# Attention score products in 32-row array tiles, row maxima by small transfers, batches run on without a break

## What is computed

```python
p = jnp.sum(c * up[None], axis=-1); z = jnp.sum(c * uz[None], axis=-1)
P = jax.nn.sigmoid(p) * key_len
Z = jax.nn.sigmoid(z) * key_len
G = -(j[None, None, None, :] - P[..., None]) ** 2 * 2.0 / Z[..., None] ** 2
scores = jnp.einsum('bhqd,bhkd->bhqk', q, k) / jnp.sqrt(jnp.float32(D))
scores = scores + G
probs = jax.nn.softmax(scores, axis=-1)
ctx = jnp.einsum('bhqk,bhkd->bhqd', probs, v)
```

## Time and profile before

| | |
|---|---|
| time, median of 3 runs | 1984.03 us |
| profiled execution, from first to last instruction | 1977.9 us |
| PE busy | 1562.8 us (79%) |
| DVE busy | 1303.5 us (66%) |
| ACT busy | 806.1 us (41%) |
| POOL busy | 344.8 us (17%) |
| first score product | 174.4 us |
| last context written | 1026.8 us |

### The profile page before, as it was taken

The page is one execution under the profiler, slowest core; times in us unless marked ns, Lnnn a source line. Parts: engine busy times, 40 slices in busy tenths (PEclk is TensorE's granted clock), DMA queues, the critical chain, the costliest instruction groups (busy, mean ns, idle before and its releaser), DMA issues. The chain is left out here.

```text
span 1977.9 us, 27765 instructions
## 1 busy us (share of the span) xinstructions
PE 1562.8 (79%) x8393; PEld 1008.6 (51%) x8393; DVE 1303.5 (66%) x2889; ACT 806.1 (41%) x979; POOL 344.8 (17%) x522
## 2 busy tenths in 40 slices
PE   4579999999999999999986804530077687999998
PEld 2245555455554555555544503420055466888887
DVE  3668888788887888788807893319754344666665
ACT  1123666566665666666673300000043333333432
POOL 0422111111111111110012203530410230000000
PEclk9867999999999999999998855555578898999999
DMA  2051000000000000000000105527000000000000
GB/s 55 0 206 50 1 1 1 2 1 1 1 1 2 1 1 1 1 1 1 1 10 22 53 11 119 129 58 289 15 0 0 1 0 1 6 7 11 6 5 11
DMA packets 38686, 53.75 MB, mean 27 GB/s; under 512 B 6032, under 2 KB 23808, under 8 KB 38555
## 3 DMA queue, kind: packets, MB, share of 16 engines
q1 hardware_dynamic: 35995, 47.62, 7.0%
q0 software_dynamic: 2560, 4.55, 1.4%
HBM read 32.93 MB, written 20.97 MB: 27 GB/s over the span
## 5 line engine op out<-in xcount | busy, mean ns | idle before, releaser
L657 DVE TENSOR_REDUCE mx<-psum 128x1 f32<-128x512 f32 x1024 | 649.1, 685 | 144.8 <-PE psum L507 144.5
L611 ACT ACTIVATE probs<-psum 128x1024 f32<-128x1024 f32 x512 | 505.1, 1024 | 312.6 <-PE psum L529 312.5
L507 PE MATMUL psum<-akT,aqT 128*128 128x512 f32 x1024 | 403.4, 446 | 5.6 <-ACT akT L592 4.7
L529 PE MATMUL psum<-aqT,akT 128*128 128x512 f32 x1024 | 331.6, 407 | 7.7 <-issue 6.2
L507 PEld LDWEIGHTS psum<-akT,aqT 128*128 128x128 f32 x1024 | 185.6, 194 | 235.9 <-DVE mx L657 160.0
L542 PE MATMUL psum<-probs,vaug 128*32 128x512 f32 x2048 | 272.8, 605 | 0.8 <-ACT probs L611 0.4
L529 PEld LDWEIGHTS psum<-aqT,akT 128*128 128x128 f32 x1024 | 186.7, 190 | 81.4 <-ACT probs L611 28.4
L2146 ACT ACTIVATE sil<-psum,moe_bg 128x512 f32<-128x512 f32 x128 | 88.0, 688 | 205.8 <-PE psum L2100 205.7
L2235 DVE SCALAR_TENSOR_TENSOR hid<-psum,moe_bu,sil 128x512 f32<-128x512 f32 x128 | 95.9, 750 | 86.4 <-ACT sil L2146 82.9
L464 POOL CAST akT<-kstage 32x512 fp32r<-32x512 f32 x120 | 73.3, 611 | 323.1 <-ACT kstage L595 317.7
L2084 PEld LDWEIGHTS psum<-down,hid 128*128 128x128 f32 x1024 | 123.6, 192 | 6.9 <-issue 1.5
(11 more groups left out here) (276 smaller groups left out, 2147.4 us busy)
## 6 DMA issues: line engine op xcount, KB each, us to landing
pick_rows<-zeros SPq DMA_DIRECT2D x48, 256.0 KB, 3.7
yk<-pick_rows SPq DMA_DIRECT2D x8, 1536.0 KB, 8.7
token_rows<-xrow SPq DMA_DIRECT2D x8, 512.0 KB, 2.8
w1b<-in_w1T SPq DMA_DIRECT2D x8, 352.0 KB
w3b<-in_w3T SPq DMA_DIRECT2D x8, 352.0 KB
w2b<-in_w2T SPq DMA_DIRECT2D x8, 352.0 KB
X<-in_x SPq DMA_DIRECT2D x4, 512.0 KB, 7.7
out<-acc SPq DMA_DIRECT2D x8, 256.0 KB, 2.3
```

The lines of the kernel that those rows point to most:

```text
L507: last = e.matmul(bank[:], qT[u % NG][:, i * P:(i + 1) * P], kT[u % NG][:, h, c * 512:(c + 1) * 512], start=True, stop=True)
L529: last = e.matmul(scores[:, n % 2, j, :], kT[g][:, h, kt * P:(kt + 1) * P], qT[g][:, hf * QH:(hf + 1) * QH], start=True, stop=True)
L611: a.activation(probs[:, n % 4, :, :], scores[:, n % 2, :, :], ACT.Exp)\
L657: dve.reduce_max(mx[:, i, h, c:c + 1], bank[:], X_AXIS).then_inc(tp_free, 1)
```

## The change

It does these things:
- `kT[u]` becomes [128, 1024], like `qT`. A score product or an X of head h takes rows 32h to 32h + 31 of both operands, so it is put into one of the array's four groups of 32 rows and uses that alone. The spreading by POOL, `kstage`, the clearing of `kT` (4 x 128 x 4096 numbers) and of `mrow` go. ACT copies K straight to `kT`.
- The X of a unit begin three steps earlier (LEAD = 3): each step has exactly four, of heads 2, 0, 3, 1, at 0.1, 0.3, 0.7 and 0.8 of the step. The last is placed 3.2 steps before the unit's scores begin, M 2.95 steps before them.
- M is one transpose of 128 x 64 to 64 x 128; ACT copies it to `mT`, and SP sends it with four transfers (one for each head, 16 pieces of 512 bytes each) to rows 30 and 31 of that head in `qT`. DVE's two additions of 128 x 512 go. The unit's first score waits for the transfers (`m_in`).
- Batches are joined: the last values and the last C of a batch stand in the first steps of the next, and the X of the next go on. The prologue has unit 0's 64 X, M, and the first 12 X of unit 1.
- SP issues three zero fills after each unit's four transfers instead of 48 at once. Counters start at 0.

```diff
-        def maxima(at, u):
-            return [(at + (2 * j + c) * 0.23, "X", u, (j // TB, j % TB, c))
-                    for j in range(GH * TB) for c in range(2)]\
-                + halves(at + 14.9, "M", u)
...
+        def maxima(v, steps):
+            lo = STEPS * (v - 1) - LEAD
             out = []
...
+            for j in range(GH * TB * 2):
+                k, r = divmod(j, 4)
+                if k in steps:
+                    out.append((lo + k + (0.1, 0.3, 0.7, 0.8)[r], "X", v, ((2, 0, 3, 1)[r], k // 2, k % 2)))
+            return out
+
+        def operands_of(v):
+            at = STEPS * (v - 2)
+            return [(at + 3.2 + 1.5 * i, "QQKK"[i], v, i % 2) for i in range(4)]
+
+        def maxima_turned(v):
+            return [(STEPS * v - LEAD + 0.05, "M", v, None)]
+
+        def context_turned(u):
+            return [(8 * u + 10.4, "C", u, None)]
...
+            with sp.Fori(0, B) as b:
+                for u in range(NG):
+                    sp.wait_ge(m_copied, b * NG + u + 1)
+                    for h in range(GH):
+                        sp.dma_start(
+                            f32(qT[u][h * R + 30:h * R + 32, :]).rearrange("l (i q) -> l i q", i=TB),
+                            f32(mT[u % 2][h * 2 * TB:(h + 1) * 2 * TB, :])).then_inc(m_in, 16)
+                    for z in range(PER):
+                        sp.dma_start(rows[:, bass.ds(((b * NG + u) * PER + z) * W, W)], zeros[:])\
+                            .then_inc(zeroed, 16)
...
+                    r = slice(h * R, (h + 1) * R)
+                    last = e.matmul(bank[:], qT[u % NG][r, i * P:(i + 1) * P],
+                                    kT[u % NG][r, c * 512:(c + 1) * 512], start=True, stop=True)
+                elif kind == "M":
+                    e.wait_ge(dve_own, (b * NG + u + 1) * M_STEPS)
+                    stand_alone(e)
+                    last = e.transpose(bank[0:GH * 2 * TB, 0:P],
+                                       f32(mrow[:]).rearrange("p h l i -> p (h l i)"), t["ident"][:])
...
-                    last = e.matmul(scores[:, n % 2, j, :],
-                                    kT[g][:, h, kt * P:(kt + 1) * P], qT[g][:, hf * QH:(hf + 1) * QH],
-                                    start=True, stop=True)
+                    r = slice(h * R, (h + 1) * R)
+                    last = e.matmul(scores[:, n % 2, j, :], kT[g][r, kt * P:(kt + 1) * P],
+                                    qT[g][r, hf * QH:(hf + 1) * QH], start=True, stop=True)
...
+                for k in range(BS):
+                    if k % STEPS == 0:
+                        e.wait_ge(m_in, (b * NG + k // STEPS + 1) * 16 * GH)
+                    score_step(b, 2 * k, first)
+                    events_to(k + 0.25)
+                    score_step(b, 2 * k + 1, first)
                     events_to(k + 0.6)
-                    if k:
-                        values_step(b, k - 1)
+                    if k or not first:
+                        values_step(b, k - 1, first)
                     events_to(k + 1)
```

More of the change, by code:

```diff
@@ new lines, in batch_events @@
+        def batch_events(first, last):
+            out = [] if first else context_turned(-1)
+            out += maxima(1, LATE) + maxima_turned(1)
+            for g in range(2, NG + 2):
+                if g < NG or not last:
+                    out += operands_of(g)
+            for g in range(2, NG):
+                out += maxima(g, ALL) + maxima_turned(g)
+            if not last:
+                out += maxima(NG, ALL) + maxima_turned(NG) + maxima(NG + 1, EARLY)
+            for u in range(2 * NG - 1):
+                out += context_turned(u)
+            if last:
+                out += [(BS + 1, "C", 2 * NG - 1, None)]
+            elif not first:
+                out += [(30.01, "-", None, None)]
+            return out
@@ L452, in build @@
[L452 to L465, removed]
@@ L565, in batch @@
                     events_to(k + 0.6)
[L566 to L567 removed]
+                    if k or not first:
+                        values_step(b, k - 1, first)
                     events_to(k + 1)
[L569 to L576 removed]
+                if last:
+                    values_step(b, BS - 1, first)
+                    events_to(BS + 2)
@@ L615, in batch @@
-                    if n % 2 and n // 2 % 8 == 0 and n > 1:
-                        context(b, n // 16 - 1)
-                context(b, 2 * NG - 1)
-            first = Events(FIRST)
-            for n, x in enumerate(FIRST):
-                if x[1] in "QK":
-                    operands(0, first, n)
-            with a.Fori(0, B - 1) as b:
-                batch(b, False)
-            batch(B - 1, True)
+                    while turns and ring.events[turns[0]][0] < k + (1 if n % 2 else 0.25):
+                        operands(b, ring, turns.pop(0))
@@ new lines, in event @@
+            def event(b, ring, n):
+                _, kind, u, at = ring.events[n]
+                bank = tp[ring.bank(n)]
+                if kind == "M":
+                    last = max(m for m in range(n) if ring.events[m][1] == "X" and ring.events[m][2] == u)
+                    dve.wait_ge(tp_free, ring.emptied(last))
+                    if ring.after is not None:
+                        dve.wait_ge(m_copied, b * NG + u)
+                    s = Steps(dve, dve_own, (b * NG + u) * M_STEPS)
+                    s.do(dve.tensor_tensor(rowmax[:], mx[:, :, :, 0], mx[:, :, :, 1], ALU.max))
+                    s.do(dve.tensor_copy(mrow[:, :, 0, :], rowmax[:]))
+                    s.done(dve.tensor_tensor(mrow[:, :, 1, :], rowmax[:], f32(mrow[:, :, 0, :]), ALU.subtract))
+                    assert s.n == M_STEPS
+                elif kind == "C":
+                    dve.wait_ge(tp_full, ring.full(n))
```

320 lines of the change are left out of this document (148 added, 172 removed).

## The result

The changed kernel takes 2009.95 us (median of 1998.7 to 2022.2) beside 1984.42 us of the kernel before in the same comparison: 1.0131 times as long, interval 1.0079 to 1.0184. The forecast was 1892 us. The profiled execution has a span of 1996.9 us against 1977.9. Of the four executions two took 1999 and 2000 us at a mean granted clock of 0.798 and 0.797, two 2020 and 2022 us at 0.786; the trace is of the fastest.

What follows compares the result with a forecast made beforehand. A loop over three banks was to bound the step at 2.70 us: 640 us, with Q, K, C, M, tail and ends 771.5 from a first score at 163.7; 92 us less gives 1892 us, own range 1860 to 1915, 1840 to 1980 at 81%.

Steps and rivals of the forecast that it cites:

- The loop of 2.70 us: Plain attention step: fourth X waits for the first's bank, values stand behind it; 237 steps of 2.70 us, 640 us.
- The pace of packed products: Eight 32-row products of a step overlap, spaced by weight loads 0.11 us apart, 0.88 us together.
- Q and K: Four groups a unit for units 2 to 15 delay the fourth X by 0.8 or 0.45 us each: 35 us.
- C: Two a unit ahead of the values, 0.8 us each; 29 in steps with X: 23 us.
- M: 15 times, TensorE waits for DVE's second X and three small steps; 2.0 us each, 30 us.
- Tail: Last 19 steps, without X: ACT's 1.85 us binds, 19 x 1.9 = 36 us.
- A cold step: Attention step at half clock: 4.4 us at most, taken as 4.1 us.
- Ahead of the first score: No clearing of `kT`, shorter normalisation, fewer K copies: first score at 163.7 us instead of 174.4.
- Changes of form paid in full: Rival, 10%: seven whole-array groups a unit each pay 0.2 us twice among packed products, 42 us: 1934 us.
- the clock's term: Half clock in the prologue and first steps only: +4 us in the sum.
- an alternating clock: Rival, 11%: steps cold a third of the time, 3.05 us a step, +83 us: 1975 us.
- a cold one: Rival, 9%: clock stays at half throughout the attention, +351 us: 2243 us.

Runs made afterwards that it cites:

- last experiment: Changed kernel with M's transpose at 0.75 of its step and four unread 128-row products into its bank ahead of it: 1891.92 us, 0.9548 of before.
- the longer wait: Changed kernel with packing undone (products over 128 rows) and DVE's first step at M done three times: 1997.94 us, 1.008 of before.
- the shorter: Changed kernel with packing alone undone (padded keys, POOL's spreading, products over 128 rows), DVE's steps at M done once: 1983.02 us, 0.9994 of before.

## Why the prediction was wrong

**The sum held, the clock did not.** The forecast put the last context at 935.2, it came at 1042.8: 107.6 us. The mean interval from one step's values to the next's is 4.50 us at half clock (the dearer steps among them) and 3.00 at full clock. So the 312 us at half clock are 312 / 4.50 = 69 intervals of 1.50 us excess each, an estimate of 104 us; a third of the time at half clock is lost. The forecast had 4 us of this, for the first steps. Of the remaining 8 us, 1.6 lie ahead of the first score and 4 in the last 19 steps (39.8 us instead of 36). With the clock held (last experiment) the stage ends at 932.4 and the kernel takes 1891.9 us. That it meets the forecast of 1892 so closely is partly luck: its first score comes 2.6 us later than the sum had it and the loop's turn isn't in the sum, while its steps with M take 3.5 to 4.5 us instead of the 4.7 summed.

By the steps of the forecast:
- The loop of 2.70 us: right. 2.69 to 2.71 in 78 of the 172 intervals at full clock, with the 0.5 us wait on a maximum at the place named and DVE idle 0.3.
- The pace of packed products: wrong in its term, without consequence. I had the eight spaced by their weight loads, 0.11 apart. Loads for different rows also start together, mostly 3 to 7 ns apart, and so do the products. The loop hides it. "TensorE: Matmul & The Clock Gate", Part 3 of the Trainium skill, gives some 4 ns from one packed product to the next and lets loads run ahead when their row groups differ; this trace agrees with both.
- Q and K: 3.3 us a step, 0.6 more, between the 0.45 and 0.8 summed. C: 3.5, 0.8 more, as summed. M: 4.4 to 4.8 at full clock, so 1.7 to 2.1 more where 2.0 was summed. Tail 2.1 a step instead of 1.9. A cold step 4.16 instead of 4.1.
- Ahead of the first score: normalisation 3.03 us instead of 13.80 (about 2.5 forecast), first X 114.9 (115.7 forecast), first score 165.3 (163.7 forecast). The four transfers issue in 2.6 us, and no wait on `m_in` shows. All right within 2 us.
- Changes of form paid in full (1934, 10%): no cost beyond the sum above is seen at Q, K and C. They aren't free: from the last transpose of a group to the next packed X or score product mostly 0.20 us pass, where the kernel before has 0.03 to its whole-array product. The sum had this in "what is left of four transposes". "TensorEngine Tiling (Array Packing)", Key Properties, of the Trainium skill says that a change of mode drains the engine; these 0.20 us agree with it, and so does the product over all rows among packed ones, which takes 0.42 to 0.44 us to the next start where products over all rows among their like take 0.23.

**The step that failed** is the clock's term. The sum has 4 us for half clock, in the first steps, and nothing behind the M's; measured are 104. I saw that the clock might fall, gave an alternating clock 11% and a cold one 9%, and worked the price out of the step's average: 0.5 of 2.70 us idle, a quarter of the array in use, set beside stretches of 10 and 20 us. The plain steps, which have just that average, keep 1.00 (181.1 to 209.9 us above, and over 350 us on end in the last experiment). What takes the clock down 15 times is the longest single wait, M's, whose 2.0 us I had summed myself and charged 30 us in all, for the wait alone. Its price in this kernel is about those 30 us and some 100 us of half clock behind it. And the earlier trace rows, from whole products, couldn't show how long packed steps stay low; the third of the time that I assumed was near the 36% measured, but I gave it too small a chance. Its 1975 us was too low all the same: it took the 83 us from the 237 plain steps alone, where the low clock lay over the whole stage.

The point from which the change loses was placed at 37% of the time at half clock, a mean clock of 0.81 in the stage. Measured: 36%, 0.81 from 400 to 600 us, and the last context 16 us later than before. So that rival had the price of a cold step and the point of no gain right within a few per cent. That they fit so well is partly luck, since it had the cause in the step's average instead of in the wait at M.

**What stays open.** Why rows count for holding the clock at M (128 rows hold it, 32 rows of the same length don't), while over the steps after a fall a 32-row product shortens the low stretches and a 128-row one doesn't. The runs exclude "one full-row product a step brings it back" and "being busy is enough"; they give no rule in its place. Nor do they show why the clock still falls at five M's when the wait there is gone. The single executions also differ: the changed kernel's times spread over 23 us, those of before over 4. The clock on record for each execution says why: 0.786 of 2018.0 us against 0.798 of 1996.9 is 864 against 807 us at half clock over the whole span, 57 us more, which at a price of a third are 19 of the 21 us between them. But only one execution of each kernel has a trace, so the counts of falls above are of one execution each. Packing with the order of before was not tried.

## What to carry to other kernels

Read the granted clock against TensorE's longest single wait in a stage and not only its busy share, above all once products use part of the array: here 2 us of waiting, 15 times, cost about 100 us beyond the waits. A gain from smaller products has to be costed twice, at either clock. The wait in such a stage is best moved (DVE's steps right behind the last maximum, the transpose 0.7 of a step later) or filled with products over all rows at that one place, not in each step. Undo the fast part and keep the rest before believing that the schedule brings anything: it was worth under 0.1% here.

## What the hardware showed that I had not expected

- Products over 32 rows of different heads start mostly 3 to 7 ns apart and so do their loads. X and scores, of different lines and banks, share the array as well as products of one group.
- After a fall at M, steps with full rows are back at 2.4 GHz in 3.4 us (six times of six with the longer wait, two of two with the shorter); packed steps stay at 1.2 GHz 24 to 31 us in ten of 15 cases.
- Eight unread products, 2.1 us in all, hold the clock when they use 128 rows (no fall at 14 M's) and mostly don't when they use 32 (10 falls of 15), at the same PE busy time.
- The turn of the batch loop leaves TensorE 2.92 to 3.57 us without a product in the five changed kernels where it came at full clock. The three packed ones then run 13.7 us at half clock, the two with full rows 3.4. The row says "issue": no wait that the profile shows.
- A product over all rows among packed ones costs 0.42 to 0.44 us of TensorE's time at full clock, where one more packed product of another head starts within 0.01.
